# A decoder layer on one core: row buffer slots renumbered, two weight pieces and one weight mix issued later

## The reference

```python
x = x + _L0_attn_ref(_layernorm(x, axis=-1), L0_attn_log_dt, ...)
...
def step(z, u_t):                      # over axis 0, 8 blocks of 64 features
    y = A * z + u_t
    z_new = jnp.einsum('hk,bpk->bph', V, y)
    return (z_new, z_new)
...
Q = (query @ Wq.T).reshape(B, T_q, N_HEADS, D_HEAD)
...
attn = jax.nn.softmax(scores, axis=-1)
out = jnp.einsum('bhqk,bkhd->bqhd', attn, V).reshape(B, T_q, D)
return out @ Wo.T
...
h = jnp.einsum('bsd,dh->bsh', x, W_exp) + b_exp
h = butterfly(h, up_weights, D_HIDDEN)
h = jax.nn.gelu(h + up_bias, approximate=False)
h = butterfly(h, down_weights, D_HIDDEN)
y = jnp.einsum('bsh,hd->bsd', h, W_con) + b_con
```

## Time and profile before

| what | value |
|---|---|
| median of 3 runs | 2243.32 us (2242.6 to 2244.34) |
| profiled execution, own time | 2245.92 us |
| its span on the core | 2244.1 us |
| granted TensorE clock, mean | 0.992 |
| TensorE busy | 2208.0 us (98%) |
| VectorE busy | 1710.0 us (76%) |
| ScalarE busy | 1230.7 us (55%) |
| GpSimd busy | 471.8 us (21%) |

### The profile page before, as it was taken

The page is one execution under the profiler, slowest core; times in us unless marked ns, Lnnn a source line. Parts: engine busy times, 40 slices in busy tenths (PEclk is TensorE's granted clock), DMA queues, the critical chain, the costliest instruction groups (busy, mean ns, idle before and its releaser), DMA issues.

```text
span 2244.1 us, 41303 instructions
## 1 busy us (share of the span) xinstructions
PE 2208.0 (98%) x15960; PEld 1938.0 (86%) x15960; DVE 1710.0 (76%) x2868; ACT 1230.7 (55%) x2749; POOL 471.8 (21%) x578
## 2 busy tenths in 40 slices
PE   8999889999999999999999999999999999999999
PEld 7788678888888888789989989989989989889899
DVE  6775588888988888857858858758669578579467
ACT  3666567766666766735536446446346356355343
POOL 3530222232322322200200300300300300201203
PEclk8999899999999999999999999999999999999999
DMA  9999613323323322476785786686676776766765
GB/s 321 338 356 307 211 60 131 119 84 123 126 86 114 123 92 90 168 244 180 217 270 172 223 269 184 214 267 208 198 259 209 226 229 208 250 207 209 227 189 194
DMA packets 202092, 443.36 MB, mean 198 GB/s; under 512 B 32442, under 2 KB 70586, under 8 KB 200362
## 3 DMA queue, kind: packets, MB, share of 16 engines
q1 hardware_dynamic: 201898, 440.72, 60.8%
HBM read 341.66 MB, written 99.01 MB: 196 GB/s over the span
## 4 chain that ended last, share of the span: by engine, by line
PE 88%; DVE 5%; DMA 3%; ACT 2%; issue 1%; SPq 0%; POOL 0%; DVEq 0%; ACTq 0%; POOLq 0%
PE ps L456 71%; PE ps L2027 5%; PE ps L1995 4%; PE ps L2006 3%; DMA x_scratch<-xa 2%; PE ps L1911 1%; PE ps L1954 1%; PE ps L1842 1%; ACT es L1106 1%; DVE st L1299 1%; DMA x<-x_scratch 1%; DVE ptl L1336 1%; PE ps L1884 0%; PE ps L1871 0%; PE ps L1807 0%
## 5 line engine op out<-in xcount | busy, mean ns | idle before, releaser
L456 PE MATMUL ps<-ring,gh 128*128 128x256 f32 x3584 | 652.8, 284 | 0.1
L456 PEld LDWEIGHTS ps<-ring,gh 128*128 128x128 f32 x3584 | 558.2, 192 | 2.2 <-DVE gl L1336 1.5
L456 PE MATMUL ps<-xth,ring 128*128 128x512 f32 x1792 | 553.4, 389 | 0.6 <-ACT U L1216 0.6
L456 PE MATMUL ps<-ring,gl 128*128 128x256 f32 x1792 | 506.8, 283 | 0.0
L456 PEld LDWEIGHTS ps<-xth,ring 128*128 128x128 f32 x1792 | 336.4, 188 | 70.7 <-issue 1.0
L1204 ACT ACTIVATE gh<-G 128x512 fp32r<-128x512 f32 x384 | 239.2, 629 | 218.8 <-PE ps L456 218.2
L456 PE MATMUL ps<-xtl,ring 128*128 128x512 f32 x896 | 348.6, 389 | 0.0
L456 PEld LDWEIGHTS ps<-ring,gl 128*128 128x128 f32 x1792 | 343.5, 192 | 0.0
L1336 DVE TENSOR_TENSOR gl<-G,gh 128x512 fp32r<-128x512 f32 x384 | 276.7, 733 | 51.2 <-ACT gh L1204 50.2
L1187 ACT ACTIVATE G<-G,up_b 128x512 f32<-128x512 f32 x192 | 138.9, 723 | 222.0 <-DVE G L1642 222.0
L1642 DVE TENSOR_TENSOR U<-ps,U 128x512 f32<-128x512 f32 (+1 forms) x167 | 136.1, 815 | 162.8 <-PE ps L456 160.1
(11 more groups left out here) (236 smaller groups left out, 4385.8 us busy)
## 6 DMA issues: line engine op xcount, KB each, us to landing
ring<-wup_scratch SPq DMA_DIRECT2D x224, 512.0 KB, 3.7
ring<-wdn_scratch SPq DMA_DIRECT2D x224, 512.0 KB, 3.6
X<-x_scratch SPq DMA_DIRECT2D x32, 1024.0 KB, 8.8
xa<-in_x SPq DMA_DIRECT2D x16, 1024.0 KB, 8.7
x_scratch<-xa SPq DMA_DIRECT2D x16, 1024.0 KB, 10.7
x<-x_scratch SPq DMA_DIRECT2D x16, 1024.0 KB, 5.6
x_scratch<-x SPq DMA_DIRECT2D x16, 1024.0 KB, 4.3
out_x<-X SPq DMA_DIRECT2D x15, 1024.0 KB, 6.3
```

The costliest lines, as they stand in the source:

```text
L456: mm = pe.matmul(bank, a, b, start=first and i == 0, stop=last and i == n - 1, skip_group_check=go_on)
```

## The change

Four edits. (1) `xslot` gives groups 0, 1, 2, 3, 4 the slots 3, 0, 4, 1, 2 in place of 3, 4, 0, 1, 2: slot 0, where `x1[0]` will lie, last holds group 11 in place of 12, and slot 4, where `wqh` will lie, group 12 in place of 11. (2) With that, `x1[0]` is loaded in quarter 1 of group 12 in place of 13; the waits for earlier row stores stand directly ahead of the next row store in groups 13 to 15; `x1[1]` is loaded behind the row store of group 14; `wqh` and `wql` are made in quarter 0 of group 15 in place of group 14. (3) Pieces 70 and 71 are made behind the first queries; group 15 keeps three. (4) `mix_weights(0)` stands behind `lo_q(3)`.

```diff
--- before.py
+++ after.py
@@ -462,11 +462,12 @@
         LU, BL, DH, UH, BH, DL = 0, MC, MC + 4, 2 * MC + 4, 3 * MC + 4, 3 * MC + 8
         YG_AT, XG_AT, YD_AT = 3, 6, 10
         PIECES = 4 * MC + 8
-        PER_GROUP = [0, 0, 6, 6, 5, 5, 5, 5, 5, 5, 5, 5, 5, 5, 5, 5]
-        assert sum(PER_GROUP) == PIECES and len(PER_GROUP) == NG
+        PER_GROUP = [0, 0, 6, 6, 5, 5, 5, 5, 5, 5, 5, 5, 5, 5, 5, 3]
+        LATE = range(PIECES - 2, PIECES)
+        assert sum(PER_GROUP) + len(LATE) == PIECES and len(PER_GROUP) == NG
         VALUES_AT = (0, 2), (1, 0), (1, 2)
         stage_turns = lambda n, i: 16 * ((n - i + STAGES - 1) // STAGES)
-        xslot = lambda g: (g + 3) % XS
+        xslot = lambda g: (3, 0, 4, 1, 2)[g % XS]
         x_turns = lambda g: 16 * (g // XS + 1)
         group_end = lambda g: sum(PER_GROUP[:g + 1])
 
@@ -601,16 +602,18 @@
                     if c == 0:
                         quarter(g)
                     if c == 1:
-                        if g:
+                        if 0 < g <= NG - 4:
                             stored(sp, x1_stored, g - 1)
                         if g and g + 4 < NG:
                             load_x(g + 4)
-                        n = g - (NG - 3)
-                        if n in (0, 1):
-                            after(sp, x1_loaded, n * 16)
-                            sp.dma_start(x1[:, n, :, :], x1_ld[n]).then_inc(x1_loaded, 16)
+                        if g == NG - 4:
+                            sp.dma_start(x1[:, 0, :, :], x1_ld[0]).then_inc(x1_loaded, 16)
+                if g > NG - 4:
+                    stored(sp, x1_stored, g - 1)
                 sp.wait_ge(x1_ready, KC * g + KC)
                 sp.dma_start(x1_st[g], xa[:, xslot(g), :, :]).then_inc(x1_stored, 16)
+                if g == NG - 2:
+                    load_x1(1)
                 if g == NG - 3:
                     sp.wait_ge(k_zero, 1)
                     load_k(0)
@@ -618,6 +621,8 @@
                     sp.wait_ge(piece_pe, UH)
                     sp.dma_start(wq_raw[:, :, :], rows(wqT)).then_inc(wq_loaded, 16)
 
+            for n in LATE:
+                piece_out(n)
             stored(sp, x1_stored, NG - 1)
             load_x1(2)
             sp.wait_ge(v_zero, 1)
@@ -1016,9 +1021,9 @@
                     if g == 2 and c == 0:
                         act.wait_ge(tup_ready, 1)
                         act.wait_ge(tdn_ready, 1)
-                    if g == NG - 2 and c == 1:
+                    if g == NG - 1 and c == 0:
                         act.wait_ge(wq_loaded, 16)
-                        act.wait_ge(x1_stored, 16 * (NG - 4))
+                        act.wait_ge(x1_stored, 16 * (NG - 3))
                         A(wqh[:, :, :], wq_raw[:, :, :], ACT.Copy, scale=SCALE).then_inc(wq_hi, 1)
                     if g == NG - 1 and c == 2:
                         apply2(0)
@@ -1031,6 +1036,8 @@
                 hi_pre(woh[:, c, :], KC + c)
                 if c == 1:
                     apply2(1)
+            for n in LATE:
+                piece_back(n)
             def apply3(g, a=0, b=T):
                 act.wait_ge(ln_ready, 2 * NG + g + 1)
                 xs = X[:, g % 2 * T:(g % 2 + 1) * T]
@@ -1409,9 +1416,10 @@
                         value_lo(1)
                     if g == 1 and c == 2:
                         bit_masks()
+                    if g == NG - 1 and c == 0:
+                        dve.wait_ge(wq_hi, 1)
+                        V.scalar_tensor_tensor(wql[:, :, :], wq_raw[:, :, :], SCALE, raw(wqh[:, :, :]), ALU.mult, ALU.subtract).then_inc(wq_lo, 1)
                 if g == NG - 2:
-                    dve.wait_ge(wq_hi, 1)
-                    V.scalar_tensor_tensor(wql[:, :, :], wq_raw[:, :, :], SCALE, raw(wqh[:, :, :]), ALU.mult, ALU.subtract).then_inc(wq_lo, 1)
                     spread2(0, range(T))
                     moments2(0)
             spread2(1, range(T))
@@ -1545,8 +1553,8 @@
                     spread2(2, range(2, T))
                     sums(3)
                     lo_q(2)
+                    lo_q(3)
                     mix_weights(0)
-                    lo_q(3)
                     return
                 lo_p(2, -1)
                 shift(0)
@@ -1944,8 +1952,9 @@
             pe.wait_ge(pre_lo, KC)
             for o in range(KC):
                 query(ps[:, o, :], o).then_inc(pre_pe, 1)
+            for n in LATE:
+                piece(n)
             pe.wait_ge(x1_ready, KC * NG)
-            pe.wait_ge(piece_act, PIECES)
 
             def turn3(p, i, bank):
                 pe.wait_ge(xn3_ready, 2 * p + (2 if p else 1 + i // 2 % 2))
@@ -2050,6 +2059,7 @@
 
                 if g == 0:
                     scores(0)
+                    pe.wait_ge(piece_act, PIECES)
                     for c in range(KC - 1):
                         turn_x(c)
                     keep_clock(5, 4)
```

## The result

The changed kernel takes 2247.24 us (median of 20 runs, 2244.09 to 2251.43), the kernel before beside it 2243.81 us (20 runs, 2239.49 to 2247.56). The ratio is 1.0018, with a 95% interval of 1.0012 to 1.0024: slower by 3.4 us, inside the 0.2% that I had called no change. The forecast was 2247.3.

A forecast was written before the change was run, and what follows sets the result against it. TensorE is busy for 98% of the span; the change reaches only its waits between stage one and attention. First scores +2.0, clock +1.0 and edit 4 +1.0 make +4.0 us: 2243.3 to 2247.3 us, 8 in 10 range 2238 to 2252.5.

The forecast's parts named there:

- First entrance: x1[0] through transposes to the queries: x1[0] loaded earlier, transposes at 227.9 to 232.0, so 3.1 to 7.2 us earlier.
- wqh and wql in group 15 cost nothing: In group 15 ScalarE and VectorE wait 6.08 and 4.95 us for landings, which would cover making wqh and wql.
- Second entrance: x1[1] to the first scores: x1[1] lands at 246.7 behind 6.0 us of added transfers; scores at 256.65, +2.0 us.
- the forecast's reading of them as transfers at about half the rate: Piece stores of 256 KB ahead of x1[1] take 1.5 us each, against 0.75 us at 353 GB/s.
- the forecast's +2.0: First scores start at 256.65 instead of 254.62, with ends +0.5 to +3.3 us.
- Clock, +1.0 us: TensorE idles ahead of the first scores, so the first attention turns run partly at half clock: +1.0 us, between 0 and 4.
- Edit 4, +1.0 us: VectorE idles 1.0 us between lo_q(2) and lo_q(3), so shift(0) and what follows come 1.0 us later.
- the work ahead of shift(0) is the same: Moving the mix behind lo_q(3) leaves VectorE's work before shift(0) unchanged, so shift(0) comes 1.0 us later.
- late pieces "at no cost": Pieces 70 and 71 behind the queries take about 1 us of TensorE, in place of a 1.65 us wait.
- The faster rival: x1[1] is not late: it lands by 239, first scores start at 249, the kernel takes 2238.6 us; chance 0.22.

The follow-up runs named there:

- e11: Changed kernel with the load of x1[1] directly ahead of the row store of group 14 instead of behind it; 2244.95 us, ratio 1.0005 to the kernel before.
- e3: Changed kernel with the load of x1[1] back in quarter 1 of group 14, ahead of two piece stores as well; 2246.74 us, ratio 1.0007 to the kernel before.
- e1: Kernel before with only mix_weights(0) moved behind lo_q(3); 2244.87 us, ratio 1.0003.
- e4: Kernel before with only the new order of the row buffer slots; 2244.35 us, ratio 0.9999.
- e5: e3 with pieces 70 and 71 back in group 15; 2241.46 us, ratio 0.9990 to the kernel before.
- e9: Changed kernel with 32 products that nobody reads ahead of the first scores, to hold the clock; 2246.85 us, ratio 1.0014 to the kernel before.
- e2: Changed kernel with mix_weights(0) put back between lo_q(2) and lo_q(3); 2247.68 us, ratio 1.0014 to the kernel before.
- e7: Kernel before with only pieces 70 and 71 moved behind the first queries; 2243.83 us, ratio 1.0000.

## Why the prediction was right, step by step

- **First entrance.** Transposes at 230.69, inside 227.9 to 232.0. Piece 68 was copied at 226.35, not at 228.5, and in the end ScalarE waited for `nmr`, the last step of the statistics, not for a piece; from their start to the transposes it took 9.4 us instead of 8.0. The 1.4 us are those of `nmr` beside `wql`, of which 0.76 stood in ScalarE's way. So "wqh and wql in group 15 cost nothing" is wrong about what runs beside them; it had no effect on the end, because the scores waited for x1[1].
- **Second entrance.** x1[1] landed at 246.7, as computed; what stands in front of it costs what the prediction said (e11: 3.4 us for the row store, against 3.0; e3: 6.2 us with the two pieces, against 6.0). The two pieces are then 1.4 us each, twice the 0.75 us that 256 KB would take at 353 GB/s. Copies that wait one behind the other for piece stores start 1.5 us apart before and 1.3 in e1, e3, e4, e5 and e9, so the forecast's reading of them as transfers at about half the rate holds. First scores at 256.54, forecast 256.65. That two numbers agree to 0.1 us is luck. The same order of transfers gave landings from 245.8 to 247.5, and the order of before gave 241.7 there and 243.56 in e1, so +5.0 us is one pair of traces, and the delay lies between 2.3 and 5.8. The first scores bear the forecast's +2.0 out: 253.50 (e4), 254.62 and 254.85 (e1) with the old place of the load, 255.66 (e2), 256.54 and 257.24 (e9) with the new one, 2.2 us apart in the mean (2.5 with e7's 252.86, which has edit 3 besides).
- **Clock, +1.0 us.** The yardstick grew by 1.5 us, of which 0.1 is edit 4: 1.4 us. e9, which keeps the clock up, takes all of it away, and 0.3 us more; before, the clock is down too, from 261.3 to 264.6. The term was undersized by 0.4.
- **Edit 4, +1.0 us.** Wrong in size: 0.1 us (e1, e2). The step "the work ahead of shift(0) is the same" was wrong about its duration: the mix beside GpSimd's multiplies takes 3.1 us, alone 2.1.
- **Edits 1 to 3, late pieces "at no cost".** Right here, but only because the scores were late as well: in the changed kernel GpSimd's clearing of `pt` starts at 262.35 and ends at 264.15, and `rinv` is done at 264.5. With earlier scores they are in the way: in e3 TensorE waits 3.27 us for GpSimd, and the yardstick is 3.9 us longer than in e5, which differs from it by these pieces alone. In e7 the clearing holds the multiply too, without a cost that the traces can tell from the clock's. I had followed them on TensorE and ScalarE and not to the engine that waits for their last store.

Sum in the traces: 1.9 at the first scores and 1.5 behind them make 3.4 us at the row maxima of group 1 (291.53 to 294.92), 3.5 us in the spans (2244.1 to 2247.6) and 3.4 us in the medians, against 4.0 predicted. The 0.6 too much are edit 4's 0.9 and the scores' 0.1, less the clock's 0.4. The faster rival named the right place, the landing of x1[1], and was incomplete too: e3 brings it to 240.5 and the gain stops at GpSimd, until the late pieces are out of its way.

## What to carry to other kernels

When a stall is moved, follow each transfer to everyone who waits for it, and count what now stands ahead of the next load in the same queue: here a load issued 11 us earlier gained 5 us for the queries, and the next one, issued 3 us later, landed 5 us later and set the end. Before a gap is moved, look at who runs beside the work that filled it, since its duration belongs to that place. The two entrances to a stage have to be shortened together: with x1[1] back in group 14, and the two pieces where their stores land before anyone waits, the same idea is 0.14% faster than the kernel before (interval 0.05 to 0.22%) instead of 0.18% slower. And a cheap step can become a long one by its neighbour alone, as `nmr` and the mix show.

## What the runs showed of the hardware

- Two fp32 elementwise streams on VectorE and GpSimd slow each other: four 128x256 additions and subtractions 2.1 us alone and 3.1 beside four 128x308 multiplies, which take 2.67 alone and 3.22 beside them. All kernels with the mix between the copies had 3.11 or 3.12 us, all with it behind them 2.07 to 2.12. A step of GpSimd on 128x4 took 0.20 us alone and 1.59 to 1.65 beside VectorE's `wql` row of 2.28.
- The hold of SyncE's queue moves to whichever transfer is next: 6.25 us on a 1 MB load before, 9.57 us on two 256 KB stores after, at the same time of the program (from 214 or 215 us). That it goes with the read of `ubs` ahead of it in the queue is argued, and wasn't tried.
- After 7.02 us without a product TensorE ran at 1.2 GHz up to 264.0 us, through scores and transposes; with products in the gap (e9) it stayed at 2.4 GHz.
